# A two-layer graph network kernel: the first layer's dense product moves out of the counting stage into the two scatter stages

## The reference

```
h  = relu(layernorm(x))
# layer(h) = concat[h, mean over in-edges of h[src], mean over out-edges of h[dst]] @ W + b
h  = relu(layer(h; W1, b1));  h = layer(h; W2, b2);  x = x + h
h  = relu(layernorm(x));  agg = segment_sum(edge_attr, dst)
x  = x + mlp(concat[h, agg, u[0]])      # leaky 256 -> leaky 256 -> 128
```

## Time and profile before

| | us |
|---|---|
| median of 3 runs | 4329.48 |
| profiled execution, its own time | 4335.07 |
| its span, first to last instruction | 4333.3 |
| TensorE busy | 3664.6 (85%) |
| VectorE busy | 3064.8 (71%) |
| ScalarE busy | 2120.2 (49%) |
| GpSimd busy | 3183.3 (73%) |
| mean granted TensorE clock | 0.946 |

### The profile page before, as it was taken

How to read it: one execution, slowest core, us unless ns; L and a number is a source line. 1 busy time by engine, 2 the same in 40 slices (tenths; PEclk the granted TensorE clock), 3 DMA queues, 4 the chain that set the end, 5 groups by cost and what they waited for, 6 DMA issues and landing times.

```text
span 4333.3 us, 98316 instructions
## 1 busy us (share of the span) xinstructions
PE 3664.6 (85%) x24032; PEld 3166.5 (73%) x24032; DVE 3064.8 (71%) x10907; ACT 2120.2 (49%) x5395; POOL 3183.3 (73%) x3256
## 2 busy tenths in 40 slices
PE   7999788888788857676666676689999999999999
PEld 5666577777777756666666666578888888888888
DVE  8999888888888833222322222279999999999997
ACT  6777633333333322222222222267777777777776
POOL 6777668888888868888888888756666666666665
PEclk9999999999999978888888888899999999999999
DMA  7888766666666758778887888766666666666664
GB/s 230 260 258 262 226 148 155 155 157 151 158 156 151 161 128 205 202 195 202 205 203 198 203 198 205 181 152 155 156 155 156 156 154 155 156 156 154 155 156 120
DMA packets 860320, 767.90 MB, mean 177 GB/s; under 512 B 204930, under 2 KB 646730, under 8 KB 860282
## 3 DMA queue, kind: packets, MB, share of 16 engines
q1 hardware_dynamic: 694074, 600.36, 45.9%
q0 software_dynamic: 166208, 167.10, 26.9%
HBM read 406.25 MB, written 309.52 MB: 165 GB/s over the span
## 4 chain that ended last, share of the span: by engine, by line
PE 38%; DMA 9%; POOL 8%; issue 6%; DVE 2%; ACT 1%; SPq 1%; DVEq 0%; POOLq 0%; ACTq 0%
PE bank L1444 8%; POOL node L612 5%; PE bank L1457 4%; PE bank L1458 4%; PE bank L1459 4%; DMA keyall<-keyrow 4%; DMA ends<-pre,index 4%; POOL ends L597 3%; PE bank L1422 2%; PE bank L1417 2%; PE bank L1415 2%; PE bank L1416 2%; PE bank L1421 2%; PE bank L1431 2%; PE bank L1339 1%
## 5 line engine op out<-in xcount | busy, mean ns | idle before, releaser
L576 POOL DMA_INDIRECT pre<-summed,rep_index x392 | 620.5, 1583 | 152.1 <-issue 115.7
L612 POOL DMA_INDIRECT node<-summed,rep_index x392 | 624.8, 1594 | 131.4 <-issue 111.3
L643 POOL TENSOR_TENSOR resid<-node_out,b3s 128x128 f32<-128x128 f32 x784 | 336.6, 459 | 506.0 <-DVE rows L1178 503.3
L1128 DVE SCALAR_TENSOR_TENSOR z<-bank,bias,small 128x512 f32<-128x512 f32 x784 | 568.2, 744 | 97.4 <-ACT small L820 93.5
L820 ACT ACTIVATE small<-bank,bias_small 128x512 f32<-128x512 f32 x784 | 536.2, 684 | 135.8 <-PE bank L1459 73.4
L1087 DVE TENSOR_SCALAR same<-keyall,keys 128x512 f32<-128x512 f32 (+3 forms) x392 | 139.8, 418 | 587.2 <-DMA keyall<-keyrow 587.2
L653 POOL TENSOR_TENSOR z_lo<-z,z_hi 128x512 fp32r<-128x512 f32 x392 | 495.8, 1285 | 9.8 <-ACT z_hi L851 9.8
L766 ACT ACTIVATE endsT<-bank,b1col 128x512 f32<-128x512 f32 x98 | 67.3, 687 | 830.9 <-PE bank L1330 830.9
L597 POOL DMA_INDIRECT ends<-pre,index x392 | 380.6, 971 | 123.7 <-issue 113.5
L1239 PE MATMUL bank<-upper,table 112*128 112x256 bf16 x2744 | 343.4, 287 | 135.7 <-DVE upper L975 135.7
L1239 PEld LDWEIGHTS bank<-upper,table 112*128 112x128 bf16 x2744 | 274.0, 103 | 195.9 <-DVE upper L975 153.5
(11 more groups left out here) (144 smaller groups left out, 9668.9 us busy)
## 6 DMA issues: line engine op xcount, KB each, us to landing
node<-blank SPq DMA_DIRECT2D x98, 768.0 KB, 5.0
rows<-in_x_dram SPq DMA_DIRECT2D x196, 256.0 KB
pre<-node_out SPq DMA_DIRECT2D x196, 256.0 KB, 4.2
rows<-pre SPq DMA_DIRECT2D x196, 256.0 KB, 5.0
normed<-in_x_dram SPq DMA_DIRECT2D x196, 256.0 KB, 6.1
y<-node_out SPq DMA_DIRECT2D x196, 256.0 KB, 2.4
node_out<-node SPq DMA_DIRECT2D x196, 256.0 KB, 3.2
node_out<-y POOLq DMA_DIRECT2D x196, 256.0 KB, 4.2
```

The source lines that it names most:

```text
L576: pool.indirect_dma_start(pre1, bass.IndirectOffsetOnAxis(ap=rep_index[:, b, s:s + 1], axis=0), summed[:, b, s, 0:F], None, compute_op=ALU ...
L612: pool.indirect_dma_start(node1, bass.IndirectOffsetOnAxis(ap=rep_index[:, b, s:s + 1], axis=0), summed[:, b, s, :], None, compute_op=ALU. ...
L1128: dve.scalar_tensor_tensor(out=z[:, m, :], in0=bank[first_bank + m][:], scalar=bias[:, m:m + 1], in1=small[:, m, :], op0=ALU.add, op1=ALU. ...
```

## The change

Stage A keeps only the counting, the gathers with their stores, and a new zero fill of the table, now called `sums1`: 512 KB on every second tick. Loads of `x`, statistics, transposes, products, scaling and the stores of `pre1` are gone from it.

Stage B gets, per group, four more fp32 matmuls and four scaled copies for the dense half of the 512 edge ends (`end_dense`, stored to `end_y`, 256 KB). The `sums` outputs share one bank.

Stage C makes the dense half of every block: statistics, normalising, transposes, and a preactivation in which the product with `W1` and the transposed `sums1` row are accumulated in one bank. The ends' rows are `sums1` gathered plus `end_dense`. The keys come from a matmul (`spread_keys`) in place of the broadcast load. The node banks, before two per kind, are single. The core of the diff:

```
 # stage A, VectorE: statistics, centring and rstd removed
-                    stats_of(...); onehots(st, 0); moments_of(...); rstd_of(...); onehots(st, 1); tensor_tensor(normed ...)
+                    for i in range(2):
+                        onehots(st, i)
 # stage A, TensorE
-                if at(2).exists: dense_products(at(2))
-                if at(1).exists: dense_transposes(at(1)); count(at(1))
+                if at(0).exists:
+                    count(at(0))
 # stage A, SyncE: load(st) and the store of pre1 removed
+                if st.exists and st.half == 0:
+                    sp.dma_start(sums1[bass.ds(st.g * FILL, FILL), :]..., zeros[:]...).then_inc(s_zeroed, 16)
 # stage B, TensorE, at the end of products(g, b)
+                    for s in range(4):
+                        last = pe.matmul(bank[5][:, s * P:(s + 1) * P], hT[:, b, s, :], W1s[:, 0, :], start=True, stop=True)
+                    last.then_inc(b_ymm, 1)
 # stage B, ScalarE, after messages(g + 1)
+                def dense_rows(g, b, uses):
+                    act.wait_ge(b_ymm, g + 1)
+                    for s in range(4):
+                        last = act.activation(end_dense[:, b, (s + 2) % 4, :], bank[5]..., ACT.Copy, scale=rstd[:, b, s:s + 1])
 # stage C, TensorE, step(g)
                     sums(g, b, uses)
+                    node_products(g, b, 0)
                     if follows:
+                        end_transposes(*ahead); x_transposes(*ahead, 0)
+                    node_products(g, b, 1)
+                    if follows:
+                        end_products(*ahead)
+                        preactivations(*ahead, uses + b, 0)
+                        spread_keys(*ahead, uses + b)
+                        x_transposes(*ahead, 1)
+                        preactivations(*ahead, uses + b, 1)
 # preactivations: bank[2], one block; waits for hx (ScalarE) and for the bank's last reader
+                    for s in range(T):
+                        pe.matmul(o, W1s[:, 0, :], hx[:, i, s, :], start=True, stop=False)
+                        last = pe.matmul(o, rows[:, q, s, :], ident[:], start=False, stop=True)
 # stage C, ScalarE, ahead(g + 1)
+                    normalised(g, b, 0)      # Sqrt, wait for shift, 4 activations 128x128 with scale and bias
+                    end_rows(g, b)
+                    normalised(g, b, 1)
+                    hidden_x(g, b, 0)        # Relu of the transposed block, 128x512
+                    end_messages(g, b)
+                    hidden(g, b, 0)          # Relu of the preactivation, 128x512
+                    hidden_x(g, b, 1)
+                    hidden(g, b, 1)
 # stage C, VectorE, step(g)
                     rep_index
+                        end_sums(g + 1); statistics(g + 1, 0)
                     dve.wait_ge(c_mm, g + 1); copies of summed(g)
+                        shifts(g + 1, 0); statistics(g + 1, 1)
+                    node_rows(g, b, uses, 0)
+                        shifts(g + 1, 1)
+                    node_rows(g, b, uses, 1)
+                        same_as(g + 1, 1 - b)
```

More of the change, by code:

```diff
@@ L344, in tick @@
                         .then_inc(a_keep[st.b], 16)
[L345 to L348, removed]
+                st = at(0)
+                if st.exists and st.half == 0:
+                    sp.dma_start(sums1[bass.ds(st.g * FILL, FILL), :].rearrange("(p r) f -> p r f", p=P),
+                                 zeros[:].rearrange("p (r f) -> p r f", f=F)).then_inc(s_zeroed, 16)
+            ticks(sp, tick, 1)
             def layer1():
@@ L421, in step, with load_x, load_sums @@
-                def step(g, b, uses):
-                    if not isinstance(g, int) or g + 1 < G:
-                        loads(g + 1, 1 - b, uses + b)
-                    stores(g, b, uses)
-                loads(0, 0, 1)
+                def load_x(g, b, i):
+                    if before(g, 2):
+                        sp.wait_ge(c_out, g * 2 + i - 3)
+                    load_block(normed, x, g, b, i, c_x)
+                def load_sums(g, b, i):
+                    if before(g, 2):
+                        sp.wait_ge(c_pre, g * 2 + i - 3)
+                    load_block(rows, sums1, g, b, i, c_load)
@@ new lines, in layer2 @@
+                sp.wait_ge(b_T, G)
+                for b in range(2):
+                    for i in range(2):
+                        load_x(b, b, i)
+                for b in range(2):
+                    sp.wait_ge(b_ykept[b], 16 * G // 2)
+                sp.wait_ge(b_mm, G)
+                for b in range(2):
+                    load_group(b, b)
+                for b in range(2):
+                    sp.wait_ge(b_done[b], 64 * G // 2)
+                for b in range(2):
+                    for i in range(2):
+                        load_sums(b, b, i)
@@ L722, in messages @@
                     last.then_inc(b_msg, 1)
+                def dense_rows(g, b, uses):
+                    act.wait_ge(b_ymm, g + 1)
+                    if before(g, 2):
+                        act.wait_ge(b_ykept[b], 16 * (uses - 1))
+                    hold(act)
+                    for s in range(4):
+                        last = act.activation(end_dense[:, b, (s + 2) % 4, :], bank[5][:, s * P:(s + 1) * P], ACT.Copy,
+                                              scale=rstd[:, b, s:s + 1])
+                    last.then_inc(b_yrows, 1)
                 def step(g, b, uses):
@@ new lines, in hidden_x, with hidden @@
+                def hidden_x(g, b, i):
+                    n = g * 2 + i
+                    act.wait_ge(c_xT, n + 1)
+                    if before(g, 1):
+                        act.wait_ge(c_pre, n - 1)
+                    act.activation(hx[:, i].rearrange("p s f -> p (s f)"), bank[3][:], ACT.Relu).then_inc(c_hx, 1)
+                def hidden(g, b, i):
+                    n, q = g * 2 + i, 2 * b + i
+                    act.wait_ge(c_pre, n + 1)
+                    if before(g, 2):
+                        act.wait_ge(c_prod, n - 3)
+                    act.activation(hT[:, q].rearrange("p s f -> p (s f)"), bank[2][:], ACT.Relu, bias=b1col[:, 0:1]).then_inc(c_hT, 1)
```

339 lines of the change are left out of this document (163 added, 176 removed).

## The result

The changed kernel takes **4471.65 us** (median of 4, 4470.06 to 4472.79), the kernel before 4329.1 in the same comparison: a ratio of 1.032, interval 1.031 to 1.0335. It is slower by 143 us.

The account below looks back on a forecast made before the run. VectorE was taken to bound A, GpSimd B and C, with C becoming a handover chain. A -212, its end -4, B +10, C +301, its start +8 and end -6 gave +97 on 4335.1: 4432, median 4426 us, range 4305 to 4530.

Parts of the forecast that it names:

- The sign: Whole kernel: slower by 2.2%, 4426 us, with C's +301 us outweighing A's -212; chance of slower 0.80.
- The chain: Stage C: handovers in a row from one `sums` to the next take 15.3 us, 15.7 with the clock, instead of 12.6.
- The rival that GpSimd stays the bound: Stage C: added work fits beside GpSimd, cycle 12.7 us, 4135 us in all, faster by 4.5%; chance 0.10.
- C's clock: Stage C: TensorE's clock taken as 0.95, lengthening its 7.9 us on the chain by 0.4 us.
- low-clock rival: Stage C: TensorE's clock stays at 0.85, cycle 16.7 us, 4523 us in all; chance 0.12.
- A tick: Stage A: 1.45 us instead of 2.53, bounds 1.3 and 1.75; over 196 ticks -212 us.
- the four limits: Stage A, per tick: GpSimd 1.37 us, DMA 1.3, ring of four `picked` buffers 1.35, VectorE at most 1.25.
- GpSimd's 1.37: Stage A, us per tick: one gather of 0.97, a gap of 0.30 and half an index copy, about 0.1.
- Saturated transfers: Stage A: the fill saturates the DMA, tick 1.75 us, 4485 us in all; chance 0.10.
- +10: Stage B: the added work costs 0.1 us per group, +10 us in all, bounds 0 and +40.

Follow-up runs that it names:

- reordered kernel: Changed kernel with the same stage C work in another program order on TensorE, ScalarE and VectorE; 4374.3 us, on another chip 4366.07 us.
- shift first: Changed kernel with VectorE making shifts(g+1, 0) in C ahead of its wait for sums(g) and the copy; 4488.87 us, on another chip 4487.64 us.
- ScalarE copies: Changed kernel with stage A's index columns copied by ScalarE instead of GpSimd; 4442.11 us.
- ring of eight: Reordered kernel plus index copies on ScalarE, with eight `picked` tiles and index columns instead of four and one store per group; 4389.71 us.
- 4170 us kernel: Changed kernel with stage C reordered on three engines and stage A's index copies on ScalarE; 4169.04 us, on another chip 4173.62 us.
- half the preactivation: Reordered kernel with the product with `W1s` left out of the node preactivations, the loaded sums alone passed through; 4196.52 us.
- index copy before the gather: Changed kernel with GpSimd in stage A copying the next group's index columns before issuing its gather, on every second tick; 4563.36 us.

## Why the prediction was right, and what in it was not

The call was slower by 2.2%, and it is 3.2%; the time lies in the range. The sign came from C, whose mechanism was right. That the time is as near as it is has luck in it: A's error is beyond its bounds, and C's, in the other direction, takes half of it back.

**C, by its steps.** Right as to mechanism. The chain was laid out at 15.3 us and is 15.32; the single steps are off by up to 0.16 us, and that they cancel is luck. `sums` to copy 3.14 (3.23 in the layout), shifts to the first activation 0.56 (0.41), each normalising 1.55 (1.54), `hidden_x` to TensorE about 0.68 (0.74), 16 passes 1.86 (1.98), keys and transposes as assumed. The reordered kernel with the index copies on ScalarE shows it from the other side: the same instructions in C in another order, 12.61 us. The rival that GpSimd stays the bound named the right cycle (12.7) for an order that this program doesn't have.

**C's clock.** Wrong by its size: I took 0.95 and 0.4 us; granted were 0.97 to 0.98, and the mean cycle is 15.35 against 15.33 in an undisturbed one. This is most of the 38 us by which C came out shorter. The rule of the Trainium skill (TensorE: Matmul & The Clock Gate, "Part 1: The HAM clock gate") that I had read for the low-clock rival, that the clock stays high while the engine is busy, would have given 39 us less, and the trace agrees with that cost, though not with a clock that is always high: the 68 cycles without a low stretch take 15.31 us in the mean, the 29 with one 15.45. With gaps of 1.9 us these stretches cost 0.1 us each, since they fell where TensorE waited anyway. With shift first they fell on the chain. The long cycle there is 1.7 us over the short one, of which 0.8 is lateness and the rest, about 0.9, the clock: the price of a low stretch depends on what it hits.

**A, the step that failed.** A tick was to be 1.45 us with bounds of 1.3 and 1.75; it was (381.9 - 17.4)/195 = 1.87, above the upper bound. Of the four limits it was GpSimd's 1.37 that was wrong, short of two terms. First, the index copy was priced at its duration, 0.1 us per tick; with the pause of 0.81 in place of a gap of 0.30 before the gather that reads it, it is (0.19 + 0.81 - 0.30)/2 = 0.35, over 196 ticks 49 us more. The kernel before, on GpSimd's timeline in A, has a `TENSOR_TENSOR` in that place, which the change removes:

```profile
203.17 0.20 POOL L508 CAST index<-keys 128x2 int32 x1
203.45 1.03 POOL L528 TENSOR_TENSOR normed<-rows,moments 128x128 f32<-128x128 f32 x1
204.63 0.98 POOL L518 DMA_INDIRECT picked<-in_x_dram,index  x1 [0.15 <-issue]
```

I had asked what the removed work costs, not what it covered; no run puts that instruction back, so the covering is read from these rows. The ScalarE copies give 28 us back. Second, gathers during the counting take 1.38 us instead of 0.96, over some 80 gathers 34 us; the earlier trace rows gave 0.97 beside a VectorE just as busy, but half of that was other work. Of the 98 us above GpSimd's 1.37 per tick these are 83. The rest, about 15 us, are waits for the stores of `picked`, for which the 0.08 us of margin in my 1.45 was enough. Saturated transfers, my case for a long tick, are refuted by a share of 0.55 to 0.68. By the rule of the Trainium skill (DMA: Bandwidth & Descriptors, "Anatomy of one DMA") GpSimd alone bounds A; the trace agrees on the engine, not on the 1.37 us that I gave it: its own instructions and pauses take 1.6 alone and 2.1 beside the counting. The page's fit is for transfers that GpSimd issues, while the fill is SyncE's, and no run here times the fill.

**B and the ends.** +5.3 for +10; waits before L1269 took in the products, as expected. The clock of B rose from 0.98 to 1.00 with it.

**Sum.** A's error of +82, C's of -38, B's of -5 and E's of +2 are +41; the median lies 1.1 us below the profiled execution and not 5.6 as before, which is another 4.5. That makes 4471 or 4472 where 4426 was forecast. A chain laid out link by link from rows of the trace came out within 0.1 us, its clock aside; a stage in which four limits lie together came out slower than each.

## What to carry to other kernels

When work moves into a stage that has slack, lay out its handovers in program order before adding busy times; where the chain is longer than the busiest engine's sum, reorder all engines together: that gave 273 us here, while a single link gave nothing on the two chips with late completions and wasn't measured on another. When you remove an instruction, ask what latency it covered. And a small copy that feeds the next DMA's index costs its handover, four times its duration here: give it to an idle engine. When a run misses, look first at a stage that the edit doesn't touch: B's length, 1039 to 1043 us or 1049 to 1068, told which runs could be compared.

## What the runs showed of the hardware

- **Late completions.** On two chips (seven runs) part of TensorE's matmul groups were reported late, in B and C and, with the ring of eight, in A. In B a fifth to three tenths of the recorded completions came over 1 us after the last issue, up to 2.5 us; in the reordered C 0.35, up to 6.1 us; in C in the changed kernel's order 0.01, and 0.06 with shift first. It is not fp32 alone: B's f16 group and its bf16 table look-up are among them. From the stages A to C of these runs 0.09 to 0.33 of the completion events are missing in the traces. In stage E, and in the other six runs (the changed kernel twice, the index copies, the 4170 us kernel twice, half the preactivation), no completion took over 0.6 us and at most 0.01 of the events are missing. It happens at a granted clock of 1.00 too (2057 to 2063 us in the reordered kernel), but B's clock is 0.93 to 0.97 in those runs and 1.00 in the others.
- **What the lateness costs, and what is open.** B took 7 to 26 us longer, and the reordered C about 150. The kernel before did not suffer by its time: 4333.8 and 4336.0 us there, 4333.0 and 4334.1 elsewhere; there is no trace of it from those chips. B's code is the same in all these runs, and the code of C is the same in the 12.6 and the 14.0 us cycle. But no kernel ran on chips of both kinds, so that it is the chip is likely and not shown; how much it costs depends on the order of the program too. What the 4170 us kernel takes on such a chip isn't known; 4366 to 4374 less the 26 us of the index copies would be about 4344, an estimate. The cause wasn't found.
- **The counting lengthens GpSimd's short work.** While VectorE writes 16-bit one-hots and TensorE counts without a break, an indirect gather is issued in 1.38 instead of 0.96 us and a copy of 128x2 in 0.33 instead of 0.20. One-hots beside a gather are not enough: in the ring of eight, where they come in bursts, the 22 gathers that had them alongside from end to end took 0.98 us in the mean, at most 1.12. Which of the two engines does it, and why only in a long run, is open.
- **A gather behind a small copy on the same engine** starts 0.81 us after the copy's end when it reads what was copied, and 0.61 when it doesn't (index copy before the gather), where indirect DMAs follow one another after 0.30.
